# Last stage of a six-layer local-attention network: TensorE's full products joined, a fourth rotary buffer, and the work at a change of layer placed elsewhere

## The chip, the cores and the metric

One NeuronCore of a Trainium2 chip runs the whole program. The metric is the time of one execution on the device in microseconds; the median of three runs stands for the kernel.

## The reference

The input is 16 sequences of 256 tokens of 128 features, in float32. Four blocks follow each other, each adding to the tokens; the last one takes two thirds of the time and is the only one the change touches. It has six layers of

```python
x = attn_layer(shift_tokens(x), Wqkv[i], q_scale[i], k_scale[i], Wo[i]) + x
x = ffn_layer(shift_tokens(x), ln_g[i], ln_b[i], W1[i], b1[i], W2[i], b2[i]) + x
```

`shift_tokens` shifts half the features by one token. The attention has 16 heads of 64, queries and keys are normalised (`q * rsqrt(sum q^2)`, times a scale), turned by rotary tables with a position-dependent factor, and each window of 32 tokens looks at itself and the window before it, under a mask, with a softmax over 64 keys. The feed-forward layer is a layer norm, `a * gelu(gate)` with 341 hidden units, and a product back.

## The kernel before, in words

The program has five instruction streams (TensorE, VectorE or DVE, ScalarE or ACT, GpSimd or POOL, and SyncE for DMAs) that meet only through semaphores. Each stream's order is written out by hand. The last stage runs 96 pieces (6 layers by 16 sequences) through a software pipeline of 100 turns. In turn f, the piece f gets its tokens and projections 0 to 4, piece f-1 projections 5 to 7, norms and keys, piece f-2 scores, softmax and token products, f-3 the attention and the feed-forward norm, f-4 the feed-forward products. The order inside a turn is the list of calls at the end of each `phase_d_` function; a call for a piece that isn't there does nothing.

What the steps are:

- `project(n, i)` on TensorE (L1910): six products of 128x128 weights with 256 columns, chunk i of eight (0 to 3 keys, 4 to 7 queries), into bank 0 or 1 in turn; the same bank must have been read by `rotary_products(n, i-2)` (semaphore `s_rp`). `squares(n, i)` on ScalarE (L1680) reads it into a square, `rotary_products(n, i)` on VectorE (L1448) multiplies it with the tables into one of `KS` buffers `d_t`, `rotary_sums` on GpSimd (L1835) adds the halves, `add_halves` on GpSimd (L1843) adds the squares, and SyncE's DMAs (`place_queries`, `place_keys`) bring the results into place.
- `sum_squares`, `norm_rsqrt`, `norm_weight`, `norm_factor`, `norm_high`, `norm_split` (L1469), `spread_norms` and `scale_keys` (L1484) make the norms and scale the keys; `turn_factors` keeps the factors for the queries.
- `scores(n, h)` on TensorE (L1943 the mask, L1950 the products), `softmax_maximum` (L1490), `softmax_shift` (L1496) on VectorE, `scale_shifted` on GpSimd (L1852), `softmax_exp` on ScalarE (L1696), `softmax_sum`, `softmax_reciprocal` on VectorE, `softmax_scale` on GpSimd, `turn_probabilities` on VectorE, `attention` on TensorE (L1995). h is the half of the piece's windows.
- `token_products(n, w)` on TensorE (L1977): tokens of window w times the head matrices `m_vo`, into banks 5, 4, 5, 4, 5, 5, 4, 5 for w = 0 to 7; `read_products(n, w)` on ScalarE (L1704) empties the bank. Product w = 2 waits until window 0 has been read.
- the feed-forward part: `residual`, `ffn_tokens` (L2006 on TensorE), `ffn_mean` (L2017), `ffn_var` (L2023), `ffn_rsqrt`, `ffn_weight` (L1529), `ffn_factor` (L1535), `ffn_scale`, `ffn_shift`, `ffn_up` (L2037), `ffn_gelu`, `ffn_gate` (L1549), `ffn_down` (L2050), `ffn_residual` (L1557). `turn_tokens` (L1897) of the next turn writes bank 6, which `ffn_residual(f-4)` reads.

TensorE uses three shapes: products over the whole array (128*128 in the rows), products in column tiles of 32 (128*32; scores, attention, token products, sums of squares), and the head matrices in row halves of 64 (64*128).

At a change of layer four things are made anew: `weights_high` (ScalarE, L1752) and `split_low` (GpSimd, L1415) round the projection weights into a high and a low part, `tables` (ScalarE, L1764) make the rotary tables, and `head_matrices` (TensorE L2064, ScalarE L1773) make `m_vo`. Tables and roundings fall into the first turn of a layer (`fresh`) and the one before it (`next_fresh`), the head matrices into the third.

## Time and profile before

| | us |
|---|---|
| median of 3 runs (4238.14 to 4240.38) | 4239.45 |
| the profiled execution | 4246.35 |
| its span, first to last instruction | 4244.5 |
| TensorE busy | 3910.8 (92%) |
| VectorE busy | 3529.0 (83%) |
| ScalarE busy | 2638.6 (62%) |
| GpSimd busy | 2381.6 (56%) |
| mean granted TensorE clock, of full speed | 0.964 |

The last stage begins near 1323 us. Matmuls are pipelined, and the profile models their ends, so starts are the sounder reading: the next block's start tells when the engine came to it. On VectorE and ScalarE consecutive instructions overlap in the trace by some 0.08 to 0.1 us.

### The profile page before, as it was taken

To read this page: it belongs to the slowest core of one execution; us is meant where nothing else is said; L and a number is where in the kernel's file an instruction comes from. 1 tells how busy PE (TensorE), PEld (TensorE's weight loads), DVE (VectorE), ACT (ScalarE), POOL (GpSimd) and SP (SyncE) were. 2 spreads that over 40 slices of the span, in tenths; PEclk is the share of its full clock that TensorE was granted. 3 is DMA by queue.
4 is the path that set the end of the run, shared out by engine and by line. 5 is a ranking of instruction groups with operands and counts; after the bars stand their busy time and mean duration, and the time that the engine had idled before them with its cause. 6 is when DMAs were issued, how large, how long until landed. Compare 5 with 4: busy or idle time off the path is not lost.

```text
span 4244.5 us, 120128 instructions
## 1 busy us (share of the span) xinstructions
PE 3910.8 (92%) x48128; PEld 2747.8 (65%) x48128; DVE 3529.0 (83%) x5537; ACT 2638.6 (62%) x5550; POOL 2381.6 (56%) x2045
## 2 busy tenths in 40 slices
PE   3457999999995999999999999999999999999998
PEld 1225776767764676667766676667766676667666
DVE  6875556777776899989998899989998899989897
ACT  3543336666664666666667666666666666666665
POOL 0111001000003787878888788878888787878785
PEclk7678999999997999999999999999999999999999
DMA  3000000000001333333332333333332333333332
GB/s 104 0 0 1 1 1 1 1 0 0 0 1 40 76 90 82 69 76 88 78 78 65 79 88 81 70 75 94 73 81 62 81 87 81 71 73 72 91 77 65
DMA packets 264482, 238.94 MB, mean 56 GB/s; under 512 B 31524, under 2 KB 260136, under 8 KB 263208
## 3 DMA queue, kind: packets, MB, share of 16 engines
q1 hardware_dynamic: 263976, 231.82, 23.5%
q8 instruction: 363, 5.95, 0.6%
q14 instruction: 143, 1.17, 0.1%
HBM read 26.20 MB, written 4.19 MB: 7 GB/s over the span
## 4 chain that ended last, share of the span: by engine, by line
PE 73%; DVE 12%; ACT 7%; issue 3%; SPq 2%; POOL 1%; DMA 1%; DVEq 0%; ACTq 0%; POOLq 0%
PE bank L1977 14%; PE bank L1910 13%; PE bank L1995 8%; PE bank L1950 7%; PE bank L2037 5%; PE bank L854 5%; ACT arena L1129 3%; PE bank L2050 2%; PE bank L1943 2%; DVE arena L1016 2%; PE bank L1921 2%; DVE arena L1026 2%; PE bank L1254 1%; SPq L2151 1%; PE bank L1245 1%
## 5 line engine op out<-in xcount | busy, mean ns | idle before, releaser
L1448 DVE TENSOR_TENSOR arena<-bank,tab 128x1024 f32<-128x1024 f32 x768 | 935.5, 1219 | 193.0 <-ACT arena L1680 138.8
L1835 POOL TENSOR_TENSOR arena<-arena 128x512 f32<-128x512 f32 x768 | 1010.7, 1332 | 49.6 <-DMA arena<-arena 44.9
L1680 ACT ACTIVATE arena<-bank 128x512 f32<-128x512 f32 x768 | 457.9, 596 | 538.9 <-PE bank L1910 530.1
L1977 PE MATMUL bank<-m_vo,arena 128*32 128x512 f32 x6144 | 757.9, 599 | 17.4 <-DVE arena L1541 11.1
L1910 PE MATMUL bank<-x_split,wqk_split 128*128 128x256 f32 x4608 | 720.7, 299 | 34.9 <-DVE arena L1448 21.0
L1910 PEld LDWEIGHTS bank<-x_split,wqk_split 128*128 128x128 f32 x4608 | 605.6, 192 | 184.3 <-issue 93.9
L1843 POOL TENSOR_TENSOR arena<-arena 128x256 f32<-128x256 f32 x768 | 558.6, 739 | 159.4 <-ACT arena L1680 158.7
L1704 ACT ACTIVATE arena<-bank 128x512 f32<-128x512 f32 x768 | 456.8, 596 | 186.9 <-PE bank L1977 184.2
L1852 POOL TENSOR_TENSOR arena<-arena 128x1024 f32<-128x1024 f32 x192 | 372.4, 1940 | 263.2 <-DVE arena L1496 263.2
L1187 POOL TENSOR_TENSOR x_all<-x_all,arena 128x256 f32<-128x256 f32 x16 | 11.6, 727 | 836.5 <-DVE arena L1008 836.5
L1858 POOL TENSOR_TENSOR arena<-arena 128x1024 f32<-128x1024 f32 x192 | 373.5, 1946 | 127.0 <-DVE arena L1509 126.7
L1950 PE MATMUL bank<-arena 128*32 128x128 f32 x12288 | 403.7, 273 | 0.0
L1995 PE MATMUL bank<-arena 128*32 128x128 f32 x12288 | 373.6, 274 | 0.6 <-issue 0.5
L1950 PEld LDWEIGHTS bank<-arena 128*32 128x32 f32 x12288 | 345.6, 110 | 36.9 <-issue 0.5
L1995 PEld LDWEIGHTS bank<-arena 128*32 128x32 f32 x12288 | 332.7, 110 | 32.5 <-issue 2.0
L1977 PEld LDWEIGHTS bank<-m_vo,arena 128*32 128x32 f32 x6144 | 159.5, 109 | 260.1 <-ACT arena L1704 140.6
L1129 ACT ACTIVATE arena<-bank,arena 128x256 f32<-128x256 f32 x512 | 235.4, 472 | 130.9 <-DVE arena L1016 128.7
L2037 PE MATMUL bank<-arena,w 128*128 128x256 f32 (+1 forms) x1152 | 282.0, 381 | 0.8 <-ACT arena L1735 0.8
L1516 DVE STREAM_TRANSPOSE arena<-arena 128x1024 f32<-128x1024 f32 x192 | 235.1, 1224 | 25.8 <-POOL arena L1858 25.8
L1490 DVE TENSOR_REDUCE arena<-bank 128x16 f32<-128x1024 f32 x192 | 234.1, 1219 | 12.0 <-PE bank L1950 4.1
L1484 DVE TENSOR_TENSOR arena<-arena,bank 128x1024 f32<-128x1024 f32 x192 | 232.1, 1209 | 3.0 <-PE bank L1932 3.0
L1496 DVE TENSOR_TENSOR arena<-bank,arena 128x1024 f32<-128x1024 f32 x192 | 233.0, 1214 | 0.0
(258 smaller groups left out, 7159.4 us busy)
## 6 DMA issues: line engine op xcount, KB each, us to landing
arena<-arena SPq DMA_DIRECT2D x1536, 128.0 KB, 2.5
wqk_stage<-in_wqk SPq DMA_DIRECT2D x6, 1024.0 KB, 8.6
out_x<-x_all SPq DMA_DIRECT2D x7, 512.0 KB, 6.0
wvt<-in_wvt SPq DMA_DIRECT2D x6, 512.0 KB, 4.4
wo<-in_wo SPq DMA_DIRECT2D x6, 512.0 KB, 5.5
arena<-in_wbh SPq DMA_DIRECT2D x1, 2048.0 KB, 9.7
w<-in_w SPq DMA_DIRECT2D x6, 341.0 KB, 5.9
wqk_stage<-out_x SPq DMA_DIRECT2D x2, 512.0 KB, 5.0
```

Source lines behind the costliest of these rows:

```text
L1448: nc.vector.tensor_tensor(d_t[c % KS].rearrange("p k h t -> p k (h t)"), bank[c % 2][:, :].unsqueeze(1).to_broadcast([P, 2, 2 * T]), tab[: ...
L1680: nc.scalar.activation(d_sq[i % 4].rearrange("p h t -> p (h t)"), bank[c % 2][:, :], ACT.Square).then_inc(s_sq, 1)
L1704: nc.scalar.activation(d_u[:, 1 + w, :, :], bank[U_BANK[w]][:, :].rearrange("p (a c) -> p a c", a=QUADS), ACT.Copy).then_inc(s_uev, 1)
L1835: nc.gpsimd.tensor_tensor(d_rot[i // 4][:, i % 4, :, :], t[:, :, 0, :], t[:, :, 1, :], ALU.add).then_inc(s_ad, 1)
L1843: nc.gpsimd.tensor_tensor(sq[:, 0, :], sq[:, 0, :], sq[:, 1, :], ALU.add).then_inc(s_sa, 1)
L1852: nc.gpsimd.tensor_tensor(e, e, factor.to_broadcast([P, WPT, QUADS, 2 * WIN]), ALU.mult).then_inc(s_rm, 1)
L1858: nc.gpsimd.tensor_tensor(d_e[h], d_e[h], d_inv[h].unsqueeze(2).to_broadcast([P, 4 * QUADS, 2 * WIN]), ALU.mult)\
L1910: last = nc.tensor.matmul(bank[c % 2][:, h * T:(h + 1) * T], wqk_split[:, i, wp, h, :], x_split[:, n % 2, xp, :], start=(q == 0), stop=(q ...
L1950: last = nc.tensor.matmul(bank[2 + b][g * WIN:(g + 1) * WIN, (2 * v + a) * P:(2 * v + a + 1) * P], d_q[:, a, g, at:at + WIN], d_k[:, a, g, ...
L1977: last = nc.tensor.matmul(bank[U_BANK[w]][g * WIN:(g + 1) * WIN, :], d_xt[n % 3][:, w * WIN:(w + 1) * WIN], m_vo[:, 4 * g:4 * g + 4, :].re ...
L1995: last = nc.tensor.matmul(bank[6][v * WIN:(v + 1) * WIN, h * C:(h + 1) * C], d_pt[h][:, at, :], d_u[:, WPT * h + v + z, r, :], start=(r == ...
L2037: last = nc.tensor.matmul(bank[UP_BANK[c]][0:m, half * T:(half + 1) * T], w1_of(n)[:, first + c * P:first + c * P + m], d_xn, start=True, ...
```

## The change

In the last stage alone:

- The number of rotary buffers, `KS`, goes from 3 to 4.
- TensorE: `project(f-1, 5)` goes from between scores and attention to directly behind `ffn_up`, and `project(f, 0, 1)` from behind the first token product to behind the third. Where the head matrices are made it stands before the first token product.
- VectorE: `rotary_products(f-1, 3)` at the turn's head becomes `rotary_products(f, 3)` behind `ffn_scale`; `softmax_maximum` of half 0 stands behind product 5; the third gate goes ahead of the second maximum; `norm_split` and the second shift go ahead of `rotary_products(f, 0)`.
- ScalarE: `softmax_exp(f-2, 0)` and `read_products(f-2, 0)` stand ahead of `norm_high` and of `squares(f, 0)`, which follows with `squares(f, 1)` behind reads 1 and 2. `ffn_rsqrt` and the second exponential go ahead of the second tables and the roundings for the next layer; the other tables and roundings are spread over the turn's first half.
- GpSimd: both `softmax_scale` stand ahead of the roundings for the next layer.
- Head matrices: halves in the order 1, 0; half 1 goes to banks 0 and 1, half 0 to banks 5 and 4, and products of the lower and upper 64 rows alternate. ScalarE copies them before the first exponential.

```diff
-        KS = 3
+        KS = 4
+        HALVES = (1, 0)
+        M_BANK = ((5, 4), (0, 1))
@@ VectorE's turn
                 turn_probabilities(f - 3, 1)
-                rotary_products(f - 1, 3)
+                rotary_products(f - 1, 4)
                 ffn_gate(f - 4, 0)
-                rotary_products(f - 1, 4)
+                rotary_products(f - 1, 5)
                 softmax_maximum(f - 2, 0)
-                rotary_products(f - 1, 5)
                 softmax_shift(f - 2, 0)
                 rotary_products(f - 1, 6, 7)
                 ffn_gate(f - 4, 1)
+                ffn_gate(f - 4, 2)
                 softmax_maximum(f - 2, 1)
                 split_low_tokens(f)
-                ffn_gate(f - 4, 2)
                 norm_weight(f - 1)
                 residual(f - 3)
                 norm_factor(f - 1)
-                rotary_products(f, 0)
                 norm_split(f - 1)
                 softmax_shift(f - 2, 1)
+                rotary_products(f, 0)
                 scale_keys(f - 1, 0)
...
                 ffn_scale(f - 3)
+                rotary_products(f, 3)
                 softmax_sum(f - 2, 1)
@@ ScalarE: head matrices
-                for g in range(4):
-                    act.wait_ge(s_m, 4 * l + g + 1)
...
-                    src = bank[5 - g % 2][:, :].rearrange("p (j c) -> p j c", j=4)
+                for i, half in enumerate(HALVES):
+                    for second in range(2):
+                        act.wait_ge(s_m, 4 * l + 2 * i + second + 1)
+                        src = bank[M_BANK[half][second]][:, :].rearrange("p (j c) -> p j c", j=4)
@@ ScalarE's turn
-                squares(f - 1, 5, 6)
+                squares(f - 1, 5)
+                if fresh:
+                    tables(layer_of(f), 0)
+                squares(f - 1, 6)
                 ffn_gelu(f - 4, 1)
+                if fresh and f:
+                    weights_high(layer_of(f), 4)
                 squares(f - 1, 7)
+                if fresh and f:
+                    weights_high(layer_of(f), 5)
                 ffn_gelu(f - 4, 2)
+                if fresh and f:
+                    weights_high(layer_of(f), 6)
                 nc.scalar.preload_act_table_set(EXP_SET)
                 norm_rsqrt(f - 1)
-                if fresh:
-                    tables(layer_of(f), 0)
-                softmax_exp(f - 2, 0)
                 if here(f - 2) and (f - 2) % SEQS == 0:
                     head_matrices(layer_of(f - 2))
-                squares(f, 0)
+                softmax_exp(f - 2, 0)
+                read_products(f - 2, 0)
                 norm_high(f - 1)
-                read_products(f - 2, 0, 1, 2)
-                squares(f, 1)
+                read_products(f - 2, 1, 2)
+                squares(f, 0, 1)
                 if fresh and f:
-                    weights_high(layer_of(f), 4, 5, 6, 7)
+                    weights_high(layer_of(f), 7)
...
                 squares(f, 2, 3)
+                ffn_rsqrt(f - 3)
+                softmax_exp(f - 2, 1)
                 if fresh:
                     tables(layer_of(f), 1)
                 if next_fresh:
                     weights_high(layer_of(f + 1), 0, 1, 2, 3)
-                ffn_rsqrt(f - 3)
-                softmax_exp(f - 2, 1)
@@ GpSimd's turn
                 add_halves(f, 0, 1, 2, 3)
+                softmax_scale(f - 2, 0)
+                softmax_scale(f - 2, 1)
                 if next_fresh:
                     split_low(pool, layer_of(f + 1), 0, 1, 2, 3)
-                softmax_scale(f - 2, 0)
-                softmax_scale(f - 2, 1)
@@ TensorE: project
+                    if n % SEQS == 2 and i < 2:
+                        pe.wait_ge(s_mvo, 4 * layer_of(n) + i + 1)
@@ TensorE: head matrices
-            def head_matrices(l, *groups):
+            def head_matrices(l):
                 pe.wait_ge(loaded_vo, 32 * (l + 1))
...
+                for half in HALVES:
+                    if half == 1:
+                        pe.wait_ge(s_rp, CHUNKS * (SEQS * l + 2))
                     else:
-                        pe.wait_ge(s_mvo, 4 * l + g - 1)
+                        at_least(pe, s_h, NF * (SEQS * l - 2) + NF)
...
@@ TensorE's turn
                 ffn_up(f - 4, 1)
+                project(f - 1, 5)
                 scores(f - 2, 0)
-                project(f - 1, 5)
                 attention(f - 3, 0)
...
-                if here(f - 2) and (f - 2) % SEQS == 0:
-                    head_matrices(layer_of(f - 2), 0, 1, 2, 3)
+                turned = here(f - 2) and (f - 2) % SEQS == 0
+                if turned:
+                    head_matrices(layer_of(f - 2))
+                    project(f, 0, 1)
                 token_products(f - 2, 0)
-                project(f, 0, 1)
                 token_products(f - 2, 1)
                 token_products(f - 2, 2)
+                if not turned:
+                    project(f, 0, 1)
                 ffn_tokens(f - 3)
```

## Rows read from the trace of the kernel before

**Rows 1.** Stretches: length; busy PE, PEld, DVE, ACT, POOL (instructions); clock; DMA share, GB/s.

```profile
2889.49:2918.69 29.20, 29.07 (x440) 20.47 (x437) 27.15 (x34) 19.78 (x37) 23.75 (x21) 1.00 0.31 72
2229.62:2259.95 30.33, 29.28 (x440) 20.45 (x436) 26.91 (x34) 21.14 (x41) 25.84 (x25) 1.00 0.34 76
2259.95:2291.64 31.69, 29.48 (x440) 20.41 (x436) 27.11 (x35) 24.14 (x50) 26.40 (x25) 1.00 0.31 68
2320.84:2354.78 33.94, 33.13 (x473) 24.11 (x469) 27.14 (x34) 22.13 (x41) 23.72 (x21) 1.00 0.28 64
1842.58:1877.99 35.41, 34.68 (x472) 24.97 (x469) 27.10 (x34) 22.14 (x41) 23.62 (x21) 0.95 0.24 55
1429.70:4140.45 2710.75, 2675.02 (x39840) 1883.55 (x39836) 2466.82 (x3006) 1839.92 (x3472) 2186.60 (x1861) 1.00 0.34 78
```

**Rows 2.** Timeline, TensorE, the ordinary turn: start, us, engine, line, shapes, count.

```profile
2891.59 0.40 PE L1943 MATMUL bank<-mask_bf,ident_bf 128*32 128x512 bf16 x4
...
2896.67 0.98 PE L1910 MATMUL bank<-x_split,wqk_split 128*128 128x256 f32 x6
...
2898.16 1.06 PE L1910 MATMUL bank<-x_split,wqk_split 128*128 128x256 f32 x6
...
2899.15 0.40 PE L1943 MATMUL bank<-mask_bf,ident_bf 128*32 128x512 bf16 x4
...
2901.34 0.61 PE L1921 MATMUL bank<-arena,sel 128*32 128x256 f32 x8
...
2901.77 1.92 PE L1995 MATMUL bank<-arena 128*32 128x128 f32 x64
...
2903.51 1.03 PE L1977 MATMUL bank<-m_vo,arena 128*32 128x512 f32 x8
...
2904.48 1.69 PE L1910 MATMUL bank<-x_split,wqk_split 128*128 128x256 f32 x12
```

**Rows 3.** Timeline, the same turn: VectorE from the first rotary product on, TensorE's `project(f, 4)`.

```profile
2906.13 1.22 DVE L1448 TENSOR_TENSOR arena<-bank,tab 128x1024 f32<-128x1024 f32 x1 [0.60 <-ACT arena L1680]
...
2908.79 1.21 DVE L1484 TENSOR_TENSOR arena<-arena,bank 128x1024 f32<-128x1024 f32 x1
...
2913.31 1.21 DVE L1448 TENSOR_TENSOR arena<-bank,tab 128x1024 f32<-128x1024 f32 x1
...
2914.62 0.42 DVE L1529 SCALAR_TENSOR_TENSOR arena<-bank,arena 128x256 f32<-128x256 f32 x1
...
2914.67 0.94 PE L1910 MATMUL bank<-x_split,wqk_split 128*128 128x256 f32 x6
...
2917.35 0.36 DVE L1557 TENSOR_TENSOR x_all<-x_all,bank 128x256 f32<-128x256 f32 x1
```

**Rows 4.** Timeline, the same turn: GpSimd and ScalarE up to the first exponential.

```profile
2899.93 0.74 POOL L1843 TENSOR_TENSOR arena<-arena 128x256 f32<-128x256 f32 x1 [0.83 <-ACT arena L1680]
...
2901.87 1.94 POOL L1852 TENSOR_TENSOR arena<-arena 128x1024 f32<-128x1024 f32 x1
...
2903.76 2.91 POOL L1835 TENSOR_TENSOR arena<-arena 128x512 f32<-128x512 f32 x2
2903.84 1.07 ACT L1696 ACTIVATE arena<-arena 128x1024 f32<-128x1024 f32 x1 [0.54 <-POOL arena L1852]
```

**Rows 5.** Timeline, first turn of a layer: read of window 0, third token product.

```profile
2277.23 0.58 ACT L1704 ACTIVATE arena<-bank 128x512 f32<-128x512 f32 x1
2277.87 0.64 PE L1977 MATMUL bank<-m_vo,arena 128*32 128x512 f32 x4 [0.24 <-ACT arena L1704]
```

**Rows 6.** Timeline, last turn of a layer: GpSimd's roundings and `ffn_factor` on VectorE.

```profile
2254.34 2.81 POOL L1415 TENSOR_TENSOR wqk_split<-wqk_stage,wqk_split 128x256 fp32r<-128x256 f32 x4
...
2256.47 0.96 DVE L1535 SCALAR_TENSOR_TENSOR arena<-arena 128x256 f32<-128x256 f32 x1
```

**Rows 7.** Timeline, third turn of a layer (starts at 2320.84): head matrices, first token product.

```profile
2334.97 3.91 PE L2064 MATMUL bank<-wo,wvt 64*128 64x128 f32 x32
...
2339.57 1.07 PE L1977 MATMUL bank<-m_vo,arena 128*32 128x512 f32 x8 [0.69 <-ACT m_vo L1773]
```

More of the change, by code:

```diff
@@ L1768, in head_matrices @@
                 act.wait_ge(s_normed, SEQS)
-                for g in range(4):
-                    act.wait_ge(s_m, 4 * l + g + 1)
-                    into = m_vo[:, :, :].rearrange("p (b j odd) c -> p b odd j c", b=2, odd=2)
-                    src = bank[5 - g % 2][:, :].rearrange("p (j c) -> p j c", j=4)
-                    nc.scalar.activation(into[:, g // 2, g % 2], src, ACT.Copy).then_inc(s_mvo, 1)
+                into = m_vo[:, :, :].rearrange("p (b j odd) c -> p b odd j c", b=2, odd=2)
+                for i, half in enumerate(HALVES):
+                    for second in range(2):
+                        act.wait_ge(s_m, 4 * l + 2 * i + second + 1)
+                        src = bank[M_BANK[half][second]][:, :].rearrange("p (j c) -> p j c", j=4)
+                        nc.scalar.activation(into[:, half, second], src, ACT.Copy).then_inc(s_mvo, 1)
             act.wait_ge(s_stats, 3)
@@ L2052, in ffn_down @@
                 last.then_inc(s_ffo, 1)
-            def head_matrices(l, *groups):
+            def head_matrices(l):
                 pe.wait_ge(loaded_vo, 32 * (l + 1))
-                for g in groups:
-                    if g < 2:
-                        at_least(pe, s_h, NF * (SEQS * l - 2) + 2 + g)
-                    else:
-                        pe.wait_ge(s_mvo, 4 * l + g - 1)
-                    d = g % 2 * DH
+                for half in HALVES:
+                    if half == 1:
+                        pe.wait_ge(s_rp, CHUNKS * (SEQS * l + 2))
+                    else:
+                        at_least(pe, s_h, NF * (SEQS * l - 2) + NF)
                     for j in range(4):
-                        a = 4 * (g // 2) + j
-                        last = nc.tensor.matmul(bank[5 - g % 2][:, j * P:(j + 1) * P], wvt[d:d + DH, a, :], wo[d:d + DH, a, :],
-                                                start=True, stop=True)
-                    last.then_inc(s_m, 1)
+                        for second in range(2):
+                            d = second * DH
+                            a = 4 * half + j
+                            last = nc.tensor.matmul(bank[M_BANK[half][second]][:, j * P:(j + 1) * P], wvt[d:d + DH, a, :], wo[d:d + DH, a, :],
+                                                    start=True, stop=True)
+                            if j == 3:
+                                last.then_inc(s_m, 1)
             pe.wait_ge(s_sel, SELS)
```

## The prediction

> All offsets below are from the start of one ordinary turn at 2889.49.
>
> **What bounds the kernel now.** I read the table of stretches first, one turn to a row: an ordinary turn takes 29.20 us, TensorE is busy for 29.07 of it at full clock, VectorE for 27.15, GpSimd for 23.75, ScalarE for 19.78 [rows 1]. From 1429.7 on, behind a slower start, 91 full turns follow before the tail, 2710.75 in all [rows 1]. Five times a layer changes, and then three turns are longer: 30.33 (turn 15 of a layer's sixteen), 31.69 (turn 0) and 33.94 (turn 2, the head matrices), the last twice of five at 35.41, with the granted clock at 0.95 [rows 1]. The other 76 are ordinary.
>
> The busy share says "TensorE"; the order of time says more. Read TensorE's row of the fifth projection chunk, `project(f, 4)`: it starts at 25.18, 0.15 after VectorE's third rotary product (23.82 + 1.21) has ended [rows 3], for the bank it writes is read by that product. So the turn is closed by a loop: the turn's start, TensorE to `project(f, 0)` at 14.99 [rows 2], the first rotary product at 16.64 (1.65 later), VectorE without a pause to 25.03 [rows 3], `project(f, 4)`, and 4.02 of TensorE to the next turn. Both engines are tight, and an edit that frees TensorE alone gives only what VectorE's half leaves.
>
> **Part 1, TensorE's order.** Between scores and attention a full block now lies: from the first mask product at 2.10 to the next full block at 7.18 are 5.08. The same two steps without a full block between take 4.36 with `sum_squares` among them (9.66 to 14.02), less its 0.43, and 0.10 more where a full block follows: 4.03 [rows 2]. That removes 1.05. Beside `ffn_up` the chunk costs its 0.99 (8.67 to 9.66 [rows 2]) less some 0.28, as the border it stands at is paid already: 0.71. Net 0.33 to 0.34 earlier for everything from `project(f-1, 6)` on. Taking `project(f, 0, 1)` out from between the token products saves two more borders, about 0.2. TensorE alone would go from 29.20 to 28.67.
>
> Those borders are TensorE's change between tile shapes. The Trainium skill, "TensorEngine Tiling (Array Packing)", Key Properties, says that changing the tiling mode drains the engine; the rows agree (about 0.1 a border). If TensorE were the only bound, as that rule invites one to think, the sum would be the first rival's.
>
> **Part 2, what `project(f, 0)` waits for.** It now stands behind three token products, and the third writes bank 5, which the first has filled: it waits for `read_products(f-2, 0)` on ScalarE. Before, 1.6 us of projection gave ScalarE that time. In the new order ScalarE runs `softmax_exp(f-2, 0)` first. Its chain: `project(f-1, 7)` at 8.67 comes 0.33 earlier, 8.34; `add_halves` behind its square 1.77 later (8.67 to 10.44 [rows 2, 4]) at 10.11; `scale_shifted` starts 1.94 after that (10.44 to 12.38) and takes 1.94, to 13.99; the exponential starts 0.03 later and ends 1.07 on, 15.09; the read begins 0.1 before that end shows, as on ScalarE throughout, takes 0.58, and ends at 15.58 [rows 4, 5]. The row of turn 0 shows that the third token product can be held just so, idle 0.24, starting 0.06 after the read's end [rows 5]. So it starts at 15.64 where TensorE alone would be there at 15.4, and `project(f, 0)` 0.97 later (14.02 to 14.99 [rows 2]): 16.61, against 16.38 unheld. Now it is at 14.99.
>
> **Part 3, VectorE behind it.** The first rotary product starts 1.65 later, 18.26. `norm_split` and the second shift are moved ahead of it, so the rest follows at once: `scale_keys` after 1.14, then 4.52 to the third rotary product (19.30 to 23.82 [rows 3]), at 23.92. `project(f, 4)` is then at 23.92 + 1.21 + 0.15 = 25.28: where TensorE's own 0.5 would put it at 24.4, it has gained nothing. From the third product to `ffn_weight` is 1.13 without the wait that makes it 1.31 now, and 2.73 to `ffn_residual` (25.13 to 27.86), plus 1.13 for the rotary product of chunk 3, which moves here from the next turn's head: 28.91, ended at 29.27 (0.36) [rows 3]. The next `turn_tokens` writes the bank that this reads: 0.15 later, **29.42**. Today that wait has 1.0 to spare. The new turn is longer by 0.22 though TensorE has 0.53 less to do. Ends: 29.19 if the third token product is not held, 29.31 if the tokens don't wait, 29.6 if that release takes 0.3. Over 76 turns: +17, ends -1 and +30.
>
> The fourth rotary buffer removes waits of VectorE for GpSimd at the turn's head, which lie outside the loop. Cost and gain nil; if GpSimd is 0.3 later it matters. GpSimd's second softmax scale comes about 1 us later (its sum waits behind the moved product); it ends near 30.95, 1.5 into the next turn, and its run of 8.28 to the last `add_halves` would reach 9.8, before 10.11. Two later steps keep their cover: `gate2` is earlier on VectorE for the second token product, and the ffn square root is done before `ffn_weight`.
>
> **Part 4, the layer's change.** Turn 15: the roundings no longer stand before the square root, so 30.33 becomes the ordinary 29.42. Turn 0: GpSimd's four low roundings (2.81 [rows 6]) now stand after both softmax scales and push the next turn's sums by 2.8, past the 0.3 that they have to spare: `project(f, 0)` at about 19.1, the turn 31.9, against 31.69. The tables move into an idle stretch of ScalarE, at nothing. Turn 2: the head products take 3.9 with each copy waited for and token products start 18.7 into the turn [rows 7]. Split over both row halves in four banks they need 3.6 if run one by one, 1.8 if two at a time (no row shows such pairs, so both ends stay). With pairs the four copies end near 17.1, the exponential and three reads follow on ScalarE before the square, the first rotary product starts near 21.5, and 11.16 on the turn ends at 32.6; one by one 34.3. I take 32.6, since all the column tiles that the trace shows run together. Before, these three were 30.33 + 31.69 + 34.53 (mean of five) = 96.55; after 93.9. Five changes: -13, ends -5 and -16.
>
> **Small terms.** The 91 turns less 76 of 29.20 and five changes of 96.55 leave 8.8 us: turns held by landing keys and by the reload of the kept tokens [rows 1]. Scores are now 0.7 later: -3 (0 to -5). The start, whose head products may pair too and which no row here prices, -3 (-8 to +2). Tail 0 (-2 to +2).
>
> **Sum.** +17 - 13 - 3 - 3 = -2. The profiled execution took 4246.35 with a span of 4244.5 and would be at 4244; on the median of the runs, 4239.45, that is **4237**.
>
> **Rivals.** (1) *TensorE is the bound* and the borders are all gained: 28.67 a turn, -40, with -16 at the changes and -6: 4177. It needs VectorE's run from `project(f, 0)` to the residual to be shorter than the rows have it. Chance 0.08. (2) *ScalarE doesn't hold the third token product*: 29.19, so -1 - 14 - 6: 4218. It needs the exponential 0.25 earlier. Chance 0.15. (3) *Slower: VectorE is late for the first rotary product.* `norm_split` now falls into the two rotary sums that end 13.99 + 2.91 = 16.9 into the turn [rows 4]. An instruction of its kind, 256 columns with two inputs in SBUF, took 0.96 while GpSimd rounded and ended 0.28 after it [rows 6]; one with an input in a bank takes 0.42 [rows 3]. So `norm_split` would end at 17.15, the shift 1.13 later, 18.2: equal with the square's 18.26. From there on it decides; 0.3 more gives 29.7 a turn, +38 - 13 - 6, so 4258. Chance 0.25. The Trainium skill, "SBUF — State Buffer", "two separate sides", states such a lock: whichever of VectorE (two SBUF inputs) and GpSimd starts first keeps the shared pair, the other blocks. The row of 0.96 agrees; by it even rival 2 would stay at 29.35, for VectorE could not be ready before 18.2. (4) *The saved border time isn't there*, the 0.2 between shapes being waits: `project(f-1, 7)` moves less and the turn is up to 29.6, within rival 3.
>
> **How the numbers follow.** The forecast 0.52, with 4228 to 4249 its own range. Faster by over 0.2% (below 4231; about what a measurement of this kernel tells from no change): rivals 1 and 2 and a little of the forecast, 0.27. Slower (above 4248): most of rival 3 and a little of the forecast, 0.26. Between: 0.47. The range takes in rivals 2 and 3 and leaves the first and the far side of the third: 4212 to 4263.
>
> **What would show it.** In an ordinary turn after: length 29.3 to 29.5; `project(f, 0)` near 16.6, just behind a read by ScalarE, and TensorE idle there; `project(f, 4)` near 25.3, still 0.15 behind the third rotary product; the first tokens 0.15 behind the feed-forward residual. Turn 15 ordinary, turn 0 not shorter, turn 2 near 32.6 with head products in pairs. It is wrong if the ordinary turn is below 29.1 (VectorE's run is not as read), or above 29.6 with VectorE ready after ScalarE's square.

## The result and the profile after

The kernel after takes 4248.57 us (median of 16 runs, 4240.86 to 4252.66), the kernel before beside it 4241.25: ratio 1.0016, 95% interval 1.0009 to 1.0024. So the change is 0.16% slower, small but clear of the noise. The forecast was 4237, 2.5 less than before; it came out 7 more. The profiled execution took 4244.35 with a span of 4242.6.

The page of the kernel after, busy shares and the chain of work that ended last:

```profile
PE 3858.0 (91%) x48128; PEld 2749.9 (65%) x48128; DVE 3596.7 (85%) x5537; ACT 2634.4 (62%) x5550; POOL 2371.6 (56%) x2045
...
PE 43%; DVE 35%; issue 10%; ACT 8%; POOL 2%; SPq 1%; DMA 0%; DVEq 0%; ACTq 0%; POOLq 0%
```

The same chain in the kernel before:

```profile
PE 73%; DVE 12%; ACT 7%; issue 3%; SPq 2%; POOL 1%; DMA 1%; DVEq 0%; ACTq 0%; POOLq 0%
```

TensorE is busy for 53 us less and the program isn't shorter: VectorE now stands beside it in the chain, with 35% instead of 12%. The table of stretches, columns as in [rows 1]; an ordinary turn, the last of a layer (15), the first (0), another first one, the third (2), and the 91 full turns:

```profile
2946.27:2975.65 29.38, 28.76 (x436) 20.68 (x437) 27.69 (x34) 19.77 (x37) 23.61 (x21) 1.00 0.32 74
2223.47:2252.85 29.38, 28.76 (x436) 20.68 (x437) 27.69 (x34) 21.00 (x41) 23.62 (x21) 1.00 0.33 74
2252.85:2286.45 33.60, 29.41 (x436) 20.70 (x437) 29.92 (x34) 24.16 (x51) 28.75 (x29) 1.00 0.28 64
3210.80:3242.79 31.99, 29.06 (x436) 20.66 (x437) 28.30 (x34) 24.40 (x51) 29.11 (x29) 1.00 0.30 67
2315.86:2348.52 32.66, 30.92 (x469) 22.50 (x469) 27.22 (x34) 21.56 (x41) 23.59 (x21) 1.00 0.30 66
1421.22:4139.35 2718.13, 2631.72 (x39840) 1891.02 (x39837) 2531.53 (x3005) 1836.18 (x3472) 2177.36 (x1861) 1.00 0.34 78
```

Against [rows 1] the 91 turns are 7.4 longer: 76 ordinary ones +13.5, five turns 15 -4.7, five turns 0 +7.9, five turns 2 -9.3. Four of the five turns 0 take 33.58 to 33.60, one 31.99. In the profiled executions the four turns ahead of these 91 gave back 4.0, the tail 0.8, and the stages that the change doesn't touch 4.5: hence a span shorter by 1.9 under a median longer by 7. The 4.5 is chance: over the thirteen kernels of this document the last stage began anywhere from 1316.4 to 1323.9. Of the gain of turns 2, 3.0 are the two at a clock of 0.95 in the kernel before. Without these two terms the profiles differ by +5.6; the medians differ by +7.3.

The ordinary turn at 2946.27, TensorE and VectorE, answering to [rows 2, 3] (timeline; L1922 is `project`, L1450 `rotary_products`, L1464 `norm_factor`, L1471 `norm_split`, L1498 `softmax_shift`, L1559 `ffn_residual`, L1907 `turn_tokens`):

```profile
2954.58 1.06 PE L1922 MATMUL bank<-x_split,wqk_split 128*128 128x256 f32 x6
...
2962.85 1.70 PE L1922 MATMUL bank<-x_split,wqk_split 128*128 128x256 f32 x12
...
2971.52 0.95 PE L1922 MATMUL bank<-x_split,wqk_split 128*128 128x256 f32 x6 [0.42 <-DVE arena L1450]
...
2975.65 0.41 PE L1907 MATMUL bank<-ident,x_all 128*128 128x128 f32 x2
```

```profile
2961.09 0.84 DVE L1464 SCALAR_TENSOR_TENSOR arena<-arena 128x256 f32<-128x256 f32 x1
2962.42 0.94 DVE L1471 SCALAR_TENSOR_TENSOR z_split<-z_split,odd,arena 128x256 fp32r<-128x256 f32 x1 [0.48 <-ACT z_split L1673]
2963.28 1.21 DVE L1498 TENSOR_TENSOR arena<-bank,arena 128x1024 f32<-128x1024 f32 x1
2964.50 1.23 DVE L1450 TENSOR_TENSOR arena<-bank,tab 128x1024 f32<-128x1024 f32 x1
...
2970.16 1.22 DVE L1450 TENSOR_TENSOR arena<-bank,tab 128x1024 f32<-128x1024 f32 x1
...
2975.14 0.36 DVE L1559 TENSOR_TENSOR x_all<-x_all,bank 128x256 f32<-128x256 f32 x1
```

Subtract 2946.27: `project(f-1, 7)` at 8.31, `project(f, 0)` at 16.58, the first rotary product at 18.23, the third at 23.89, `project(f, 4)` at 25.25 and idle 0.42 ahead of it, the residual at 28.87 to 29.23, the next turn at 29.38.

Turn 0 at 2252.85, GpSimd (L1417 the roundings, L1845 the rotary sums, L1862 `scale_shifted`) and VectorE (timeline):

```profile
2254.37 2.81 POOL L1417 TENSOR_TENSOR wqk_split<-wqk_stage,wqk_split 128x256 fp32r<-128x256 f32 x4
2257.13 2.52 POOL L1845 TENSOR_TENSOR arena<-arena 128x512 f32<-128x512 f32 x2
...
2267.32 1.94 POOL L1862 TENSOR_TENSOR arena<-arena 128x1024 f32<-128x1024 f32 x1
2269.22 2.52 POOL L1845 TENSOR_TENSOR arena<-arena 128x512 f32<-128x512 f32 x2
```

```profile
2258.52 1.23 DVE L1450 TENSOR_TENSOR arena<-bank,tab 128x1024 f32<-128x1024 f32 x1 [2.83 <-POOL arena L1845]
...
2267.75 4.28 DVE L1438 TENSOR_TENSOR x_split<-arena,x_split 128x256 fp32r<-128x256 f32 x1
...
2275.04 1.22 DVE L1450 TENSOR_TENSOR arena<-bank,tab 128x1024 f32<-128x1024 f32 x1
```

L1438 is `split_low_tokens`, a VectorE instruction with two inputs in SBUF. Such an instruction waits while GpSimd works, as rival 3 of the prediction has it: 0.41 to 0.44 when nobody is in its way, 1.14 in most turns. Here it is issued with 1.51 of GpSimd's `scale_shifted` (L1862) left, and ends not behind that, but 0.29 behind both rotary sums that follow. The first rotary product stands 22.19 into the turn instead of 18.23. In the turn of 31.99 the same instruction came in after `scale_shifted` (1.79 long). By this one turn the lost port is worth 1.6.

The head matrices, turn 2 (timeline), answering to [rows 7]:

```profile
2329.63 2.06 PE L2077 MATMUL bank<-wo,wvt 64*128 64x128 f32 x32
...
2330.88 2.07 ACT L1776 ACTIVATE m_vo<-bank 128x512 f32<-128x512 f32 x4 [1.57 <-PE bank L2077]
```

### The profile page after: what moved, and what is told of

It is laid out like the page before. It is cut to its first block, busy times and chain, and to the rows that moved or that the text cites. A ratio compares the mean times of both kernels' runs of the same rounds, so it can differ in the third digit from the quotient of the medians.

```text
span 4242.6 us, 120155 instructions
## 1 busy us (share of the span) xinstructions
PE 3858.0 (91%) x48128; PEld 2749.9 (65%) x48128; DVE 3596.7 (85%) x5537; ACT 2634.4 (62%) x5550; POOL 2371.6 (56%) x2045
## 4 chain that ended last, share of the span: by engine, by line
PE 43%; DVE 35%; issue 10%; ACT 8%; POOL 2%; SPq 1%; DMA 0%; DVEq 0%; ACTq 0%; POOLq 0%
PE bank L1922 7%; PE bank L1989 6%; DVE arena L1486 5%; PE bank L2049 5%; DVE arena L1450 5%; PE bank L854 4%; PE bank L1962 4%; PE bank L2007 4%; ACT arena L1129 3%; DVE arena L1505 3%; DVE x_split L1438 3%; DVE arena L1498 3%; DVE arena L1492 2%; DVE arena L1016 2%; DVE arena L1551 2%
## 5 line engine op out<-in xcount | busy, mean ns | idle before, releaser
L1450 DVE TENSOR_TENSOR arena<-bank,tab 128x1024 f32<-128x1024 f32 x768 | 936.1, 1220 | 105.5 <-ACT arena L1682 75.2
L1845 POOL TENSOR_TENSOR arena<-arena 128x512 f32<-128x512 f32 x768 | 1008.6, 1329 | 14.4 <-DMA arena<-arena 10.8
L1922 PE MATMUL bank<-x_split,wqk_split 128*128 128x256 f32 x4608 | 729.0, 301 | 58.9 <-DVE arena L1450 54.2
L1922 PEld LDWEIGHTS bank<-x_split,wqk_split 128*128 128x128 f32 x4608 | 613.2, 192 | 189.7 <-issue 162.0
L1862 POOL TENSOR_TENSOR arena<-arena 128x1024 f32<-128x1024 f32 x192 | 372.0, 1938 | 180.6 <-DVE arena L1498 180.6
L1498 DVE TENSOR_TENSOR arena<-bank,arena 128x1024 f32<-128x1024 f32 x192 | 233.9, 1218 | 3.3
L1698 ACT ACTIVATE arena<-arena 128x1024 f32<-128x1024 f32 x192 | 201.7, 1051 | 52.0 <-POOL arena L1862 51.9
```

The costliest lines, as they stand in the source:

```text
L1450: nc.vector.tensor_tensor(d_t[c % KS].rearrange("p k h t -> p k (h t)"), bank[c % 2][:, :].unsqueeze(1).to_broadcast([P, 2, 2 * T]), tab[: ...
L1845: nc.gpsimd.tensor_tensor(d_rot[i // 4][:, i % 4, :, :], t[:, :, 0, :], t[:, :, 1, :], ALU.add).then_inc(s_ad, 1)
L1862: nc.gpsimd.tensor_tensor(e, e, factor.to_broadcast([P, WPT, QUADS, 2 * WIN]), ALU.mult).then_inc(s_rm, 1)
L1922: last = nc.tensor.matmul(bank[c % 2][:, h * T:(h + 1) * T], wqk_split[:, i, wp, h, :], x_split[:, n % 2, xp, :], start=(q == 0), stop=(q ...
```

## The experiments

The theory after the comparison: the ordinary turn went as forecast, and turn 0 pays since GpSimd's run comes 2.8 late and `split_low_tokens` then loses SBUF's shared port to three GpSimd instructions in a row (`scale_shifted` and both sums). A table first; the turns are those of the profiled execution. "Port lost" counts the `split_low_tokens` of a run, of 96, that waited for at least one GpSimd instruction more than the one they met; the kernel before has none.

| kernel | median us | ratio to before, interval | ordinary turn | turn 0 | port lost by L1438 |
|---|---|---|---|---|---|
| after | 4248.57 | 1.0016 (1.0009 to 1.0024) | 29.38 | 33.6, one 31.99 | 5 |
| e7_roundings_spread | 4227.97 | 0.9974 (0.9964 to 0.9983) | 29.39 | 29.59 | 1 |
| e2_one_input | 4241.60 | 1.0004 (0.9994 to 1.0014) | 29.38 | 32.59 | 0 |
| e1_roundings_back | 4243.46 | 1.0009 (0.9999 to 1.0019) | 29.38 | 32.63 | 7 |
| e3_project_back | 4222.45 | 0.9957 (0.9941 to 0.9973) | 29.14 | 34.2 to 35.5 | 5 |
| e5_best | 4195.34 | 0.9899 (0.9884 to 0.9914) | 29.14 | 29.7 | 0 |
| e8_split_early | 4196.85 | 0.9901 (0.9886 to 0.9916) | 29.14 | 29.7 | 0 |
| e4_residual_first | 4294.63 | 1.0128 (1.0111 to 1.0145) | 29.44 or 30.94 | 33.7 | 43 |
| e9_residual_mid | 4222.98 | 0.9960 (0.9944 to 0.9975) | 28.90 | 29.5, 34.4, 35.4 | 12 |
| e10_split_between | 4234.95 | 0.9980 (0.9962 to 0.9999) | 28.90 | 29.5, one 34.5 | 17 |
| e11_gpsimd_waits | 4177.19 | 0.9852 (0.9835 to 0.9868) | 28.90 | 29.7 | 0 |
| b1_ks4 | 4235.71 | 0.9995 (0.9986 to 1.0004) | 29.21 | 31.7 | 0 |

### Turn 0: where the roundings stand

**e7_roundings_spread**, the kernel after with:

```diff
                 softmax_scale(f - 2, 0)
+                if next_fresh:
+                    split_low(pool, layer_of(f + 1), 0, 1)
                 softmax_scale(f - 2, 1)
-                if next_fresh:
-                    split_low(pool, layer_of(f + 1), 0, 1, 2, 3)
@@ next turn
+                if fresh:
+                    split_low(pool, layer_of(f), 2, 3)
                 scale_shifted(f - 2, 1)
```

> The changed kernel, with GpSimd's four low roundings for the next layer taken apart: two between the two softmax scales, two in the next turn between the rotary sums and the second shifted scale. Theory: the first turn of a layer takes 33.6 us because the roundings push GpSimd's run of sums by 2.8 us, and VectorE's split of the tokens then loses the shared port to three GpSimd instructions in a row (4.27 us instead of 1.15). With the run no longer pushed the turn takes 29.4 to 29.8 and the whole is 19 to 21 us shorter than the changed kernel. Rival: the turn is long through ScalarE's tables and roundings in its first half; then it stays above 32 and the whole within 8 us of the changed kernel. Ordinary turns 29.38 by both.

Measured: 20.6 less than after. Turn 0 and its `split_low_tokens`:

```profile
2249.29:2278.88 29.59, 28.80 (x437) 20.72 (x437) 27.90 (x34) 24.46 (x51) 28.01 (x27) 1.00 0.33 74
```

```profile
2262.38 1.15 DVE L1438 TENSOR_TENSOR x_split<-arena,x_split 128x256 fp32r<-128x256 f32 x1
```

The same instructions, two of them 15 us later in the turn, and it loses its 4.0. By the turn of 31.99, 1.6 of that are the lost port; the other 2.4 are the late run itself. The place of four instructions of 0.7 us decided the sign of the whole change.

**e2_one_input** makes `split_low_tokens` a copy with one input, so that it doesn't need the port; the subtraction is left out.

```diff
-                nc.vector.tensor_tensor(x_split[:, n % 2, 1, :], d_xt[n % 3], x_split[:, n % 2, 0, :].bitcast(F32), ALU.subtract)\
-                    .then_inc(s_split, 1)
+                with nc.allow_low_precision(reason='probe'):
+                    nc.vector.tensor_reduce(out=x_split[:, n % 2, 1, :], in_=d_xt[n % 3].unsqueeze(2), op=ALU.add, axis=AXX).then_inc(s_split, 1)
```

> The changed kernel, with the low half of the split tokens written by an instruction with one SBUF input (a reduction over an axis of one); the subtraction is left out, so the projections' low products work on other numbers. Theory (the port is kept by GpSimd against a VectorE instruction with two SBUF inputs): that instruction takes about 0.4 us everywhere, the first turn of a layer falls from 33.6 to about 32, no ordinary turn is above 30.5, the ordinary turn stays at 29.38, since there the instruction's wait of 0.9 is hidden; 8 to 12 us shorter than the changed kernel. Rival (the long instructions are a symptom, and GpSimd's late run sets the turn itself): the first turn stays at 33.6, the whole within 3 us.

Measured: 7.0 less than after, where 8 to 12 were expected; the intervals of the two ratios overlap, so how much it is stays open. Its turns 0 fell to 32.6, where about 32 was expected, and give 3.4 of it. VectorE in a turn 0 (timeline):

```profile
2271.65 0.41 DVE L1439 TENSOR_REDUCE x_split<-arena 128x256 fp32r<-128x256 f32 x1
...
2272.87 3.05 DVE L1464 SCALAR_TENSOR_TENSOR arena<-arena 128x256 f32<-128x256 f32 x1
```

The copy takes 0.41 and waits for nobody; the next instruction with two SBUF inputs, `norm_factor` (0.41 alone), pays instead: 3.05, issued with 0.29 of `scale_shifted` left and held through both sums, in all five turns 0, and for one GpSimd instruction more in three ordinary turns, which take 29.9 to 30.1. So the loss isn't tied to one instruction of VectorE, but to GpSimd's run standing where VectorE has such instructions. Ordinary turns stayed at 29.38: the 1.15 of the split there cost nothing.

**e1_roundings_back**: all four roundings ahead of both scales, as before the change.

> The changed kernel with the four low roundings for the next layer ahead of both softmax scales on GpSimd, as the kernel before had them; weights_high on ScalarE stays behind the second exponential. Theory (what costs turn 0 its 4 us is that GpSimd's run in it comes 2.8 us late, whatever the order in front of it): turn 0 stays at 32 to 34 us, and turn 15 grows as the first scale now waits for the roundings: 0 to 10 us slower than the changed kernel. Rival (the order of scales and roundings itself is the cause): turn 0 falls below 31 and the kernel is 8 us or more faster than the changed kernel.

Turn 0 fell only to 32.63, inside the theory's range; that turn 15 would grow was wrong (29.39), and the whole came out 5.1 below after, not 0 to 10 above, though the intervals overlap. GpSimd there:

```profile
2249.28 2.81 POOL L1417 TENSOR_TENSOR wqk_split<-wqk_stage,wqk_split 128x256 fp32r<-128x256 f32 x4 [1.67 <-ACT wqk_split L1754]
2252.05 3.76 POOL L1868 TENSOR_TENSOR arena<-arena 128x1024 f32<-128x1024 f32 x2
```

GpSimd was idle for 1.67 ahead of them, for they round what ScalarE's `weights_high` writes, which the change moved behind the second exponential; and a first scale that ends late is needed only in turn 0. The run is still late, and L1438 lost the port in all five turns 0, issued with 1.52 to 1.54 left. The order on GpSimd alone is not the cause. e7_roundings_spread shows what is: all four in one block ahead of turn 0's run.

### The ordinary turn: where `project(f, 0, 1)` stands

**e3_project_back**, the kernel after with `project(f, 0, 1)` behind the first token product again, and what belongs to it:

```diff
                 token_products(f - 2, 0)
+                if not turned:
+                    project(f, 0, 1)
                 token_products(f - 2, 1)
                 token_products(f - 2, 2)
-                if not turned:
-                    project(f, 0, 1)
@@ ScalarE
-                read_products(f - 2, 0)
+                squares(f, 0)
                 norm_high(f - 1)
-                read_products(f - 2, 1, 2)
-                squares(f, 0, 1)
+                read_products(f - 2, 0, 1, 2)
+                squares(f, 1)
@@ VectorE
+                rotary_products(f, 0)
                 norm_split(f - 1)
                 softmax_shift(f - 2, 1)
-                rotary_products(f, 0)
```

> The changed kernel, with the projections 0 and 1 back behind the first token product, and what uses them back in the order of before (ScalarE: squares 0 ahead of the reads; VectorE: rotary product 0 ahead of the norm's split and the second shift). Projection 5 stays beside the feed-forward product. Theory (the turn is a loop through the first projection and VectorE's run behind it): projection 0 at 14.7, the first rotary product at 16.3, the feed-forward residual ended at 28.85, the turn 29.0: 0.4 us shorter than the changed kernel though TensorE has two more changes of shape; 28 to 34 us shorter in all, and some 20 shorter than before. Rival (TensorE's changes of shape are what counts): the turn is 0.2 longer, 29.6.

Ordinary turns fell by 0.24 to 29.14, 0.13 short of the 29.0 expected, and turns 2 from 32.66 to 31.38. The turn at 2932.62:

```profile
2947.25 1.69 PE L1922 MATMUL bank<-x_split,wqk_split 128*128 128x256 f32 x12
...
2961.25 0.36 DVE L1559 TENSOR_TENSOR x_all<-x_all,bank 128x256 f32<-128x256 f32 x1
...
2961.76 0.41 PE L1907 MATMUL bank<-ident,x_all 128*128 128x128 f32 x2 [0.22 <-DVE x_all L1559]
```

`project(f, 0)` is at 14.63, 1.95 earlier than in the kernel after, and the turn gets 0.24 of it: now the next tokens are idle 0.22 for the residual. Its turns 0 are worse (34.2 to 35.5, five losses): `project(f, 0)` reads the split tokens, and this early in the turn TensorE itself stands still for them. TensorE in the turn at 2245.02:

```profile
2264.23 2.88 PE L1922 MATMUL bank<-x_split,wqk_split 128*128 128x256 f32 x12 [2.63 <-DVE x_split L1438]
```

**e5_best** is this with the roundings of e7:

> The kernel of e3_project_back (project(f,0,1) behind the first token product) with the roundings spread as in e7_roundings_spread: two low roundings between the two softmax scales, two in the next turn ahead of the second scale_shifted. Theory (turn 0 of a layer pays because three GpSimd instructions stand in a row when split_low_tokens comes): turn 0 falls from 34.2-35.5 us to about 29.4, five times, so 26 us less than e3_project_back: about 4196, a ratio of 0.990 to the kernel before, and ordinary turns stay at 29.13. Rival (turn 0 is long for another cause, such as the tables or the key transfers of the new layer): turn 0 stays above 32 and the time is within 10 us of e3_project_back, above 4210.

4195.34, 27 less than e3_project_back where 26 were expected, and turns 0 of 29.7: both gains are there, the rival is out.

**b1_ks4**: the kernel before with `KS = 4` alone.

> The kernel before with a fourth rotary buffer and nothing else. Theory (VectorE's waits for GpSimd at the turn's head lie outside the loop that closes the turn): ordinary turns stay at 29.20, the time within 2 us of the kernel before. Rival: VectorE's waits for a free buffer pass on into the turn, or the freed VectorE collides with GpSimd on the shared port: a change of over 4 us in either direction.

No change that the runs can tell, as said for "cost and gain nil": ordinary turns 29.21, against 29.20. The medians differ by 3.4, more than the theory's 2 and less than the rival's 4, but the interval takes in 1 and single executions go from 4230 to 4248.

### The residual, and the port again

**e4_residual_first**: the kernel after with `ffn_residual(f-4)` ahead of the second sum and reciprocal.

> The changed kernel, with the feed-forward residual ahead of the second softmax sum on VectorE. Theory: the last thing late in an ordinary turn is that residual, 0.14 ahead of the next tokens; the fifth projection stands only 0.1 behind it. So the turn falls from 29.38 to 29.26, not more, 8 to 11 us in all. The second reciprocal is 0.3 later, and GpSimd's run has 0.24 to spare; where it hasn't, single turns of 31 become more frequent and take the gain back. Rival (the residual isn't what the next turn waits for): 29.38 unchanged.

A clear miss: 46 slower than after. An ordinary turn without a loss took 29.44, where 29.26 was expected, and of the 96 `split_low_tokens` 43 lost the port. One of each kind, VectorE:

```profile
2590.97 3.76 DVE L1438 TENSOR_TENSOR x_split<-arena,x_split 128x256 fp32r<-128x256 f32 x1
...
2986.87 1.29 DVE L1438 TENSOR_TENSOR x_split<-arena,x_split 128x256 fp32r<-128x256 f32 x1
```

The residual's place makes GpSimd's second scale, and so its run in the next turn, later by up to 0.2; `split_low_tokens` then has 1.0 to wait instead of 0.86. Almost half of the turns lose 2.5 there (3.76 against 1.29), and 1.5 of it reaches the turn's end.

**e8_split_early** takes e5_best and issues `split_low_tokens(f)` ahead of the second `softmax_maximum`.

> e5_best with split_low_tokens moved ahead of softmax_maximum(f-2,1): it is issued near 11.96 us of the turn, when GpSimd's rotary sum of chunk 5 has about 0.1 us left, not 1 us or more of the following scale_shifted. Theory (the loss of the port grows with the time that the waiting instruction has to wait): split_low_tokens takes under 0.7 us in every turn, no turn is lost to it; ordinary turns stay at 29.13, 2 to 4 us below e5_best. Rival: the later start of scale_shifted (0.25 to 0.3 us) delays the exponential, the read of window 0 and so the whole turn by up to 0.3 us: plus 20 us over e5_best.

No losses, and 0.41 in the median (1.14 at most), but no gain over e5_best, which had lost none either: my 2 to 4 us were not there.

**e9_residual_mid** is e8_split_early with `ffn_residual(f-4)` between sum and reciprocal.

> e8_split_early with ffn_residual(f-4) between softmax_sum and softmax_reciprocal of half 1. In e3_project_back the turn ended at 29.13 only since turn_tokens of the next turn waits for that residual (0.14 us behind it) while TensorE's own work after project(f,4) would end at 28.8. Theory (two loops, the residual's and TensorE's, and the residual's is the longer one): the turn falls to about 28.84, 26 us less than e8_split_early, about 4167. Rival: GpSimd's softmax scale of half 1 comes 0.3 to 0.45 us later, its run in the next turn goes with it and the freed time comes back as losses of the shared port or as VectorE waiting for GpSimd: within 8 us of e8_split_early or above it.

Both happened. Two ordinary turns, one without and one with a loss:

```profile
2934.39:2963.29 28.90, 28.77 (x439) 20.61 (x437) 26.14 (x35) 19.66 (x37) 23.70 (x20) 1.00 0.30 68
2551.60:2583.35 31.75, 29.06 (x436) 20.59 (x437) 30.46 (x35) 19.66 (x38) 23.19 (x20) 1.00 0.30 68
```

The turn is 28.90 where nothing happens: with the residual out of the way TensorE's own 28.87 (28.67 and the two borders of 0.2 in all that this order pays again) is the bound. The trace shows TensorE without a wait in this turn, while VectorE is busy for 26.14. But 12 turns lose the port, and TensorE waited 14 times, 29.4 in all, for `split_low_tokens`. One of them, GpSimd and VectorE:

```profile
2562.55 1.27 POOL L1845 TENSOR_TENSOR arena<-arena 128x512 f32<-128x512 f32 x1
...
2563.56 4.89 DVE L1438 TENSOR_TENSOR x_split<-arena,x_split 128x256 fp32r<-128x256 f32 x1
...
2563.79 1.92 POOL L1862 TENSOR_TENSOR arena<-arena 128x1024 f32<-128x1024 f32 x1
...
2565.68 2.48 POOL L1845 TENSOR_TENSOR arena<-arena 128x512 f32<-128x512 f32 x2
```

Only 0.26 of the sum at 2562.55 were left, and VectorE waited through three more instructions.

**e10_split_between** moves `split_low_tokens(f)` between the second and the third gate, where 0.64 would be left.

> e9_residual_mid with split_low_tokens moved between the gates of the second and third third, so that it is issued near 11.6 us of the turn, when GpSimd's rotary sum has 0.64 us left instead of 0.27. In e9_residual_mid split_low_tokens lost the shared port in 12 of 93 turns, each time through three to five GpSimd instructions; over all runs so far nearly all losses fall where the wait would have been 0.26-0.28, 1.00-1.04, 1.26-1.28 or 1.50-1.54 us, and none of about 15 with 0.40 to 0.82. Theory (the loss hangs on the moment, not on the length of the wait, and nothing else held up e9_residual_mid): no losses, ordinary turns at 28.90 as in the undisturbed turns of e9_residual_mid, 18 to 22 us less than e5_best: about 4175, ratio 0.985. Rival (the residual moved into the sum's place makes GpSimd's run later, and with that VectorE loses the port somewhere whatever the place): at least 8 losses, 4190 or more.

Wrong: 17 losses, up to 6.66 us long. That 0.40 to 0.82 was safe stood on 15 cases.

**e11_gpsimd_waits** is e9_residual_mid with GpSimd made to wait:

```diff
+                if here(f):
+                    pool.wait_ge(s_split, f + 1)
                 scale_shifted(f - 2, 0)
```

> e9_residual_mid with one wait more: GpSimd starts scale_shifted(f-2,0) only when split_low_tokens(f) has ended, so that at the end of the rotary sum ahead of it nothing of GpSimd's can pass VectorE by. Theory (all that e9_residual_mid and e10_split_between lose is the port won by GpSimd at that one place): split_low_tokens takes 0.55 us in every turn, no loss there; scale_shifted starts 0.4 us later but takes 1.94 instead of 2.14, so the first exponential ends near 15.65 us, just in time for the square of chunk 0; ordinary turns 28.90 to 29.0, about 4170 to 4178, ratio 0.985. Rival 1 (the longest wait moves on: norm_factor or norm_split lose the port instead): turns of 28.90 mixed with turns 1 us longer or more, above 4190. Rival 2 (the later exponential pushes the square of chunk 0): all turns near 29.1 to 29.2, 4190 to 4200.

GpSimd and VectorE in the turn at 2903.04 (timeline), the next turn as a stretch, and `split_low_tokens` over the whole run (count, then shortest/median/longest in ns):

```profile
2914.00 1.28 POOL L1845 TENSOR_TENSOR arena<-arena 128x512 f32<-128x512 f32 x1
...
2915.12 0.44 DVE L1438 TENSOR_TENSOR x_split<-arena,x_split 128x256 fp32r<-128x256 f32 x1
...
2915.64 1.94 POOL L1862 TENSOR_TENSOR arena<-arena 128x1024 f32<-128x1024 f32 x1 [0.37 <-DVE x_split L1438]
```

```profile
2932.06:2960.96 28.90, 28.77 (x440) 20.62 (x437) 26.26 (x35) 19.67 (x37) 23.47 (x20) 1.00 0.35 80
```

```profile
L1438 DVE TENSOR_TENSOR x_split<-arena,x_split x96: 409/548/1143, 1318.7 to 4080.8; 128x256 fp32r<-128x256 f32 x96
```

In e9_residual_mid this last row reads 408/548/6270. GpSimd idles 0.37 for it, no turn is lost, an ordinary turn takes 28.90 (the one at 2932.06), and the kernel is at 4177.19: 1.5% faster than before, 46 less than the same kernel without the wait. Rival 1 shows only once, in the tail, where a `norm_factor` took 2.74; both rivals are out.

## Why the prediction was wrong, by its steps

- **The loop** was read rightly: `project(f, 4)` still follows the third rotary product, by 0.14 where it was 0.15.
- **Part 1** held: `project(f-1, 7)` at 8.31 (8.34 forecast). That TensorE alone would reach 28.67 is borne out by e9_residual_mid and e11_gpsimd_waits, at 28.90 with two borders more.
- **Part 2** held: `project(f, 0)` at 16.58 (16.61); the read of window 0 starts at 14.95 and ends at 15.52 (15.58). The third token product starts 0.06 behind that, at 15.58, and 0.2 later than the even steps of the products ahead of it: it was held, though too briefly for the profile to print a wait.
- **Part 3** held: first rotary product 18.23 (18.26), third 23.89 (23.92), residual 28.87 (28.91), turn 29.38 (29.42). So +13.5 for the 76 turns, where I had +17. e3_project_back shows the price of the moved `project`, with the orders on ScalarE and VectorE that went with it: 0.24 a turn, beyond which the residual holds the turn.
- **Part 4**: turn 15 at 29.38 (29.42) and turn 2 at 32.66 (32.6) held, the latter step by step: 32 head products in 2.06 instead of 3.91, copies ended at 17.09 (17.1), first rotary product at 21.50 (21.5). **Turn 0 is the step that failed.** I had GpSimd's delay right and took only its way over the exponential; for that way alone the forecast was right, as the turn of 31.99 shows: `project(f, 0)` at 19.03 (19.1 forecast), the first rotary product at 20.68. In the other four `project(f, 0)` is at 19.23 because it waits for the split tokens, done at 19.17, and the first rotary product follows only at 22.19, for all of VectorE's work behind the split is late. That other way, VectorE's `split_low_tokens` inside a longer wait for the port, I had put at nothing without following it. I priced turn 0 at +0.2; it was +1.9 where the port was lost (33.60 against 31.69), and the one turn that won it was 31.99. Five turns: +7.9 instead of +1, more than the whole gain that was forecast. e7_roundings_spread takes 18 of these turns' us away at once.
- **Small terms**: the irregular turns were to give 3; the excess over 76 even turns is 8.5, as before (8.7), one of them a lost port worth 2.0. The start gave 4.0 (3 forecast).
- **The sum**, forecast to measured: -2, then +7 for turn 0, +3 for the irregular turns, +3 for the clock, -3.5 for the ordinary turns, -2 for start and tail: +5.5, against +7.3 between the medians; where the other 1.8 lie is open. The clock's 3.0 sat in my mean of turn 2, of which the median need have nothing. The profiled execution hid the misses: its first stages and its clock were by chance 7.5 better than those of before.
- **Rival 3** had the right mechanism at the wrong place: `norm_split` took 0.94 and ended 0.28 after GpSimd, as said, and was level with the square. What it lacked is that the port can be lost more than once. Its last sentence, that VectorE couldn't be ready before 18.2, also means that rival 2's turn was 29.35 and not 29.19. **Rival 2** did not occur. **Rival 1** did not either: a turn bound by TensorE came only with the reorderings of e11_gpsimd_waits, at 28.90 and 4177.19; that this is the 4177 of the rival is chance, for the two are added up from other terms. **Rival 4** is out with Part 1.

## What to carry to other kernels

When a step is moved on GpSimd, list every VectorE instruction with two SBUF inputs that falls into GpSimd's new run, and price it at the whole rest of the run, not at the end of the instruction that it meets. Where such an instruction must sit inside a run, make GpSimd wait for it: 0.37 idle bought 46 us here. And before believing that a faster half shortens a loop, ask who is second: here the residual's release held back TensorE's 0.24.

## What the runs showed of the hardware

**The shared port doesn't queue.** A waiting VectorE instruction that gets the port ends 0.28 after GpSimd's instruction (1.14 where 0.86 was left). But GpSimd's next instruction, if it is ready, can take the port ahead of it, and then each further one too: 3.76, 4.28, 4.89 and 6.66 us were seen for 0.41 of work. Over the thirteen traces I set the outcome against what was left of GpSimd's instruction when VectorE's was issued (the four instructions with two SBUF inputs, `split_low_tokens`, `norm_factor`, `norm_split` and `ffn_factor`, GpSimd working on without a gap; the few with over 1.55 left are not in it):

| left, us | cases | lost |
|---|---|---|
| under 0.25 | 403 | 3 |
| 0.26 to 0.29 | 134 | 17 |
| 0.30 to 0.60 | 580 | 0 |
| 0.60 to 0.67 | 94 | 16 |
| 0.68 to 0.98 | 621 | 1 |
| 0.99 to 1.03 | 72 | 37 |
| 1.04 to 1.25 | 313 | 9 |
| 1.26 to 1.47 | 18 | 5 |
| 1.48 to 1.55 | 26 | 19 |

The losses stand in narrow bands and not at long waits as such: the kernel before met the port with 1.06 to 1.08 left in most turns, longer than the 0.86 of the kernel after, and lost none. But a band is mostly one place in the program: about 500 of the 580 cases at 0.30 to 0.60 are `norm_factor`, and all but a few at 0.99 to 1.03 are `split_low_tokens` of e4_residual_first. So time left and place aren't told apart. The bands were drawn from the same data, and e10_split_between shows what a forecast from them is worth; what makes them is open. What was tested is that GpSimd's wait ends it. The Trainium skill, "SBUF — State Buffer", "two separate sides", says that whichever starts first keeps the pair for its whole instruction; the rows agree, and add that the one who waits has no claim on the next turn.

**Row halves run in pairs**: 32 head products alternating between lower and upper 64 rows took 2.06, and their starts come two at a time, a pair every 0.11. In the kernel before they come one every 0.11 in groups of eight of the same rows, 3.91 in all [rows 7]; waits for copies can be no more than some 0.4 of that, the wider steps between the groups.

**A stall can bring the clock with it.** The five turns 0 of e3_project_back, in each of which TensorE is idle for over 4.4, took 34.2 three times at a granted clock of 1.00, and twice, as here, 1.3 more at a mean of 0.95. In both of these the clock fell to 1.2 from 2.4 GHz for 3.41 us, 0.1 and 1.2 after TensorE had started again behind the idle 2.63 shown above. Twelve products took 2.88 instead of 1.69 there and, in the other turn, the token products behind them 3.24 instead of 1.92. The same stall went without a fall three times; what decides is open. The whole turn, and the stretch of the fall, columns as in [rows 1]:

```profile
2245.02:2280.57 35.55, 31.05 (x437) 21.79 (x437) 29.96 (x34) 24.24 (x51) 28.74 (x29) 0.95 0.26 58
```

```profile
2264.33:2267.74 3.41, 3.41 (x16) 2.69 (x20) 2.09 (x5) 1.39 (x3) 0.00 (x0) 0.50 0.66 144
```
